# Mode weights turned to column order during the convolutions, and mixed as the moving operand

## The reference, cut to what matters

```python
# layer 0: three 3x3 convolutions whose weights are mixed per sample
x = x + conv3(conv2(conv1(gn(x))))     # w1..w3 = softmax(...) mix of 4 experts
# layer 1: a Hartley transform, cut to its middle 64 x 64 modes
X = dht2d(gn(x));  Xr = flip_periodic(X)          # h = Re fft2 - Im fft2
x_even, x_odd = (Xc + Xrc) / 2, (Xc - Xrc) / 2    # c: the middle 64 x 64
total = einsum('bixy,ioxy->boxy', x_even, weight) \
      + einsum('bixy,ioxy->boxy', x_odd, flip_periodic(weight))
x = x + dht2d(pad(total), inverse) + bias
```

## Time and profile before

| | |
|---|---|
| runs | 4752.64 us, median of 3 (4747.78 to 4760.87) |
| profiled execution | 4754.18 us; its span in the trace is 4752.4 us |
| convolutions | 0 to 3256 us |
| forward transform | 3257 to 3797 us |
| mixing | 3797 to 4056 us |
| inverse transform | 4056 to 4752 us |
| busy, share of the span | PE 91%, ACT 69%, DVE 61%, POOL 47% |
| HBM | read 746.67 MB, written 293.88 MB |

### The profile page before, as it was taken

One profiled execution on the slowest core, in us unless ns is written; L12 is line 12 of the kernel. 1 busy time (PEld: TensorE's weight loads), 2 busy tenths in 40 slices (PEclk: granted clock), 3 DMA queues, 4 the chain that ended last, 5 costly groups with the idle time before them and its releaser, 6 DMA issues. The chain is left out here.

```text
span 4752.4 us, 121017 instructions
## 1 busy us (share of the span) xinstructions
PE 4324.2 (91%) x40114; PEld 2695.9 (57%) x40114; DVE 2883.4 (61%) x4306; ACT 3292.8 (69%) x6385; POOL 2241.6 (47%) x2115
## 2 busy tenths in 40 slices
PE   4999999999999999999999999996677656899998
PEld 2555555454454555545555555454677656788887
DVE  4555555555555555555555555555699866565555
ACT  3888888888888888888888888884466567333333
POOL 4455454554545545455454554545799765000000
PEclk9999999999999999999999999998899978999999
DMA  4867768676686766867668676687999899899999
GB/s 136 198 153 180 171 150 198 153 180 169 151 197 152 180 168 151 197 153 180 167 153 199 155 179 163 157 198 208 301 320 323 272 205 205 336 409 411 409 404 378
DMA packets 717207, 1041.90 MB, mean 219 GB/s; under 512 B 151808, under 2 KB 599072, under 8 KB 667168
## 3 DMA queue, kind: packets, MB, share of 16 engines
q1 hardware_dynamic: 683296, 1032.09, 78.0%
q10 hardware_dynamic: 33792, 8.65, 1.0%
HBM read 746.67 MB, written 293.88 MB: 219 GB/s over the span
## 5 line engine op out<-in xcount | busy, mean ns | idle before, releaser
L350 PE MATMUL bank<-ring_B,w_now 128*64 128x512 f16 (+1 forms) x14283 | 3088.6, 377 | 58.3 <-DVE w_now L558 47.8
L350 PE MATMUL bank<-ring_A,w_now 128*64 128x512 f16 (+1 forms) x14283 | 3088.5, 377 | 0.0
L350 PEld LDWEIGHTS bank<-ring_B,w_now 128*64 128x64 f16 x14283 | 1551.6, 109 | 1484.0 <-DVE w_now L558 55.9
L350 PEld LDWEIGHTS bank<-ring_A,w_now 128*64 128x64 f16 x14283 | 1551.5, 109 | 52.5
L571 DVE SCALAR_TENSOR_TENSOR ring_A<-bank,ring_A 128x512 f16<-128x512 f32 (+1 forms) x1027 | 696.8, 678 | 1140.0 <-ACT ring_A L418 1119.9
L288 ACT COPY ring_B<-ring_A 64x516 f32<-64x516 f32 x1590 | 988.1, 621 | 503.0 <-DVE ring_A L571 434.3
L290 ACT COPY ring_B<-ring_A 64x516 f32<-64x516 f32 x1059 | 658.5, 622 | 12.3
L721 POOL TENSOR_TENSOR ring_A<-xn,ring_A 128x512 f16<-128x512 f32 x515 | 582.7, 1131 | 94.5 <-POOL xn L719 89.4
L418 ACT ACTIVATE ring_A<-bank 128x512 f16<-128x512 f32 (+1 forms) x1027 | 600.0, 584 | 35.7 <-PE bank L350 25.9
L1502 DVE SCALAR_TENSOR_TENSOR i_ot<-i_ob,i_bias_bc,i_xt 128x512 f32<-128x512 f32 x512 | 366.1, 747 | 288.0 <-DMA i_xt<-x 144.7
L1446 PE MATMUL i_ob<-i_back,i_u 128*128 128x256 f32 x2048 | 529.1, 381 | 7.9 <-DVE i_ot L1502 4.5
(11 more groups left out here) (163 smaller groups left out, 4982.0 us busy)
## 6 DMA issues: line engine op xcount, KB each, us to landing
f_xt<-x SPq DMA_DIRECT2D x128, 1024.0 KB, 6.9
i_xt<-x SPq DMA_DIRECT2D x128, 1024.0 KB, 16.0
out<-i_ot SPq DMA_DIRECT2D x128, 1024.0 KB, 14.2
st_in_A<-in_x SPq DMA_DIRECT2D x65, 1024.0 KB, 7.4
st_in_B<-in_x SPq DMA_DIRECT2D x65, 1024.0 KB, 7.9
x_in_A<-in_x SPq DMA_DIRECT2D x324, 192.0 KB, 3.9
res_A<-in_x SPq DMA_DIRECT2D x324, 192.0 KB, 5.2
res_B<-in_x SPq DMA_DIRECT2D x324, 192.0 KB, 5.1
```

The lines of the kernel that those rows point to most:

```text
L350: last = nc.tensor.matmul(dst[64 * half:64 * half + 64, 0:nb * IMG], w_now[n][:, w, 64 * dx:64 * dx + 64], r[side][:, kind, s0:s0 + nb, dx ...
```

## The change

Four parts.

1. In the convolutions, per sample s, SP loads four rows y of the weights (`w_rows`, in the tile `first`; four DMAs, each of 32 partitions and 32 pieces of 256 B per partition, 4096 pieces in all). DVE turns them to column order [x, o] by eight copies of 128 x 512 (four straight, in the inner loop at t = 5; four reversed, at t = 27, 28, 30, 31), and SP stores the two results to a DRAM tensor `turned` (two DMAs of 128 partitions, 8 KB pieces, 1 MB each). DVE waits once per sample, right after step 2, for all four loads.
2. The forward high parts are all made by ACT (two per group); ACT no longer copies half of y, and DVE copies both halves. The DRAM tensor `modes` is [2, 2, C, M/2, S, M]: the pieces of 256 B that SP stores lie 4 KB apart along a row index, where before they lay side by side.
3. The mixing loads `m_wt` directly from `turned` (16 DMAs of 32 partitions per chunk, 8 KB pieces), and `m_f_raw` in 16 KB pieces. The masked modes are the stationary operand and the weights the moving one. ACT and DVE build `m_ft`, one half each; POOL has no part; neither `m_raw` nor its copies exist. The result goes out in one DMA of 128 partitions with 8 KB pieces per chunk, by SP.
4. The inverse stage's constants are loaded by SP during chunk 3 of the mixing.

```diff
@@ build_convs, SyncE @@
             with sp.Fori(0, S) as s:
                 nxt = sp.snap((s + 1) % S)
                 n0 = sp.snap(s * NCH)
+                sp.wait_ge(turned, s * 8 + 1)
+                for j in range(4):
+                    sp.dma_start(w_rows[j * C:(j + 1) * C, :, 0:M], mode_w[:, :, bass.ds(s * 4 + j, 1), :].rearrange("i o a x -> i o (a x)")
+                                 ).then_inc(rows_here, 16)
...
                     load_stat(buf, nxt2, g - 1)
+                sp.wait_ge(turned, s * 8 + 9)
+                for i in range(2):
+                    sp.dma_start(turned_d[i, bass.ds(s * 4, 4)].rearrange("y i x -> (y i) x"), w_cols[i].rearrange("p x o -> p (x o)")
+                                 ).then_inc(turned_out, 16)
                 sp.wait_ge(x1_ready, n0 + NCH + 1)
@@ build_convs, VectorE @@
+            def turn_rising(i):
+                cols = bass.ds(i * 16, 16)
+                nc.vector.tensor_copy(w_cols[0][:, cols, :], w_rows[:, :, cols].rearrange("p o x -> p x o")).then_inc(turned, 1)
...
                 step(n0, 2, ("C", 0, s, None))
+                dve.wait_ge(turned_out, s * 32 + 1)
+                dve.wait_ge(rows_here, s * 64 + 64)
+                chain(nc.vector.tensor_copy(w_rows[:, :, M], w_rows[:, :, 0]), nb)
+                dve.sem_inc(passed, 1)
...
+                        if t == 5:
+                            turn_rising(i)
...
+                    if t in (27, 28, 30, 31):
+                        turn_falling((27, 28, 30, 31).index(t))
@@ load_weights @@
+    p = slice((2 * part + half) * C, (2 * part + half + 1) * C)
+    for t in range(ROWS):
+        r = ROWS * k + t
+        y = (M - r if half != part else r) if r else M // 2 * half
+        engine.dma_start(wt[p, t, :], turned_d[part, y]).then_inc(here, 16)
@@ build_forward @@
-        fv = f_d.rearrange("m t s (g c) r x -> m t s (c r) g x", c=4)
+        fv = f_d.rearrange("m t (g c) r s x -> m t s c r g x", c=4)
...
-                copy_y(nc.vector.tensor_copy, 0, g).then_inc(y_dve, 1)
+                nc.vector.tensor_copy(y_mid[:, :, 4 * g:4 * g + 4], made[:, :, :, NH - 1])
+                for wc in range(2):
+                    last = nc.vector.tensor_copy(y[buf][:, wc], made[:, wc, :, 0:M].rearrange("p c (t k) -> p t c k", t=2))
+                last.then_inc(y_ready, 1)
@@ build_forward, ScalarE @@
+                for j in range(2):
+                    part = lambda t: t[:, 2 * j:2 * j + 2, :].rearrange("p c w -> p (c w)")
+                    ch = 4 * g + 2 * j
+                    nc.scalar.activation(part(xh[g % NX]), part(xt[g % NX]), ACT.Copy, scale=scale_now[even][:, ch:ch + 1]
+                                         ).then_inc(hi_ready, 1)
@@ build_mix, SyncE @@
+            for k in range(NCK):
                 if k >= 2:
+                    sp.wait_ge(ft_dve, (k - 1) * NQ)
+                    sp.wait_ge(ft_act, (k - 1) * NQ)
+                load_modes(k)
+                if k >= 2:
+                    sp.wait_ge(made, (k - 1) * NQ)
+                    for part in range(2):
+                        for half in range(2):
+                            load_weights(sp, turned_d, k, part, half, wt[k % 2], w_here[k % 2])
+                    store(k - 2)
+                if k == 3:
+                    sp.dma_start(back[:], spec[:, OFF_BACK:OFF_BACK + 2 * IMG]).then_inc(consts_here, 16)
@@ build_mix, TensorE @@
-                    last = nc.tensor.matmul(bank[n % 2][:, x, :], wt[:, kx, :], ft[:, kx].rearrange("p t g b -> p (t g b)"),
+                    last = nc.tensor.matmul(bank[n % 2][:, x, :].rearrange("p (t o) -> p t o", t=T),
+                                            ft[:, kx].rearrange("p t g b -> p (t g b)"), wt[k % 2][:, :, kx * C:(kx + 1) * C],
                                             start=True, stop=True)
```

More of the change, by code:

```diff
@@ L127, in build_convs @@
         first = sb("first", [P, 8, 512 * 4])
+        spare = first[:].rearrange("p a b -> p (a b)")
+        w_rows = spare[:, 0:C * (M + 1)].rearrange("p (o x) -> p o x", o=C)
+        w_cols = [spare[:, 2048 * (2 + i):2048 * (3 + i)].rearrange("p (x o) -> p x o", o=C) for i in range(2)]
         bank = [[ps(f"bank{n}{i}", [P, 512]) for i in range(2)] for n in range(3)]
@@ L276, in _ @@
             sp.wait_ge(stored_stats, 16)
+            sp.wait_ge(turned_out, 32 * S + 1)
         def taps_view(m, n, dx):
@@ L1235, in _ @@
-                        sp.dma_start(to_rows(own, T - own), rows(T * k + own, T - own)).then_inc(f_here[buf], 16)
-                if k >= 2:
-                    sp.wait_ge(re_ready, (k - 1) * NQ)
-                    sp.wait_ge(im_ready, (k - 1) * NQ)
-                    for i in range(4):
-                        load_weights(sp, w, k, i, raw[buf], w_here[buf])
+                            sp.dma_start(f_raw[k % 2][p, 0], fm_d[:, :, part * M:(part + 1) * M].rearrange("b i x -> i b x")).then_inc(f_here[k % 2], 16)
@@ L1328, in _ @@
+            act.wait_ge(masks, 1)
             for n in range(NQ):
-                real(n)
+                modes(act, 1, n, multiply).then_inc(ft_act, 1)
             for n in steps:
-                take(act, nc.scalar.copy, (1, 2, 3), n, taken_act)
+                take(act, nc.scalar.copy, (2, 3), n, taken_act)
                 if n + NQ in steps:
-                    real(n + NQ)
-                if n >= NQ and n % NQ == 0:
-                    store(n // NQ - 1)
-            store(NCK - 1)
+                    modes(act, 1, n + NQ, multiply).then_inc(ft_act, 1)
@@ L1343, in _, with build_inverse @@
             last.then_inc(masks, 1)
-            pool.wait_ge(masks, 1)
-            for n in range(NQ):
-                modes(pool, nc.gpsimd.tensor_scalar, 0, n).then_inc(ft_pool, 1)
-            for n in steps:
-                if n + NQ in steps:
-                    pool.wait_ge(made, n + 1)
-                    modes(pool, nc.gpsimd.tensor_scalar, 0, n + NQ).then_inc(ft_pool, 1)
-def build_inverse(nc, t_d, x1d, bias, spec, out_d, S):
+def build_inverse(nc, t_d, x1d, back, bias_bc, out_d, S):
     f32 = mybir.dt.float32
@@ L1512, in build @@
     x1_stats = scratch("x1_stats", [P, S, 2])
[L1513 to L1515 removed]
+    modes, middle = scratch("modes", [2, 2, C, M // 2, S, M]), scratch("middle", [S, C, 2 * M])
+    mixed_modes = scratch("mixed_modes", [M // 2, 2, S, C, M])
+    turned = scratch("turned", [2, M, C, M * C])
+    build_convs(nc, x, w_c1, w_c2, weight1, weight2, weight3, mode_w, turned, consts, x1, x1_stats, S)
     with ExitStack() as ctx:
[L1518 to L1522 removed]
+        sb = lambda name, shape: ctx.enter_context(nc.sbuf_tensor(name, shape, f32))
+        back, bias_bc = sb("i_back", [P, 2 * IMG]), sb("i_bias_bc", [P, C])
+        with ExitStack() as inner:
+            wt = [inner.enter_context(nc.sbuf_tensor(f"m_wt{i}", [P, ROWS, M * C], f32)) for i in range(2)]
+            build_forward(nc, x1, x1_stats, spec, modes, middle, turned, wt, S)
+            build_mix(nc, modes, middle, turned, mixed_modes, wt, back, bias_bc, spec, bias, S)
+        build_inverse(nc, mixed_modes, x1, back, bias_bc, out, S)
 _INS = ["x", "L0_conv_w_c1", "L0_conv_w_c2", "L0_conv_weight1", "L0_conv_weight2", "L0_conv_weight3",
```

200 lines of the change are left out of this document (62 added, 138 removed).

## The result

The changed kernel takes 4897.97 us (median of 4 runs, 4891.78 to 4906.95) against 4750.21 for the kernel before on the same chip: ratio 1.0308, 95% interval 1.0284 to 1.0333. The forecast was 4807 us (range 4712 to 4900): the right side, but 57 us more were forecast where 148 us came. The execution that was profiled spans 4890.0 us, 137.6 more than before.

The account below looks back on a forecast made before the run. PE was taken to bound the convolutions, DVE and DMA the forward stage, DMA the mixing. 128 - 37 - 36 - 1 = +54 on 4754.2 gave 4808, less 1.5 for the median: 4807 us, range 4712 to 4900.

Parts of the forecast that it names:

- PE loses 8.4 - 1.9 = 6.5 us: Convolutions, each sample boundary: DVE's 8.1 us wait plus 0.3 for column copy and semaphore, less PE's 1.9 in hand.
- the new stretch at 1.2 GHz: Convolutions, after each boundary stop: 3.4 us of PE at the low clock, costing 1.7 us, taken once more.
- Rivals B and C: B: rows land before DVE wants them, 4684 us, chance 0.07; C: 256 B pieces cost like 1 KB, 5010 us, 0.08.
- The 5 us forecast behind the last sample: End of convolutions: the queue empties 5 us later, ahead of the forward stage; part of the +128 us.
- I charge nothing: Convolutions: the eight turning copies per sample, 0.47 to 0.92 us each, were taken to cost no time.
- the bound of 115: Convolutions: cost of the turning copies if nothing covers them, 128 x 0.9 = 115 us.
- The cover that was named: Convolutions: DVE's 1.9 us idle in a step and PE's 1.9 us in hand were to absorb the turning copies.
- the 3.29 us: Forward stage: DVE's time per group, 3.75 - 0.87 + 0.41; 3.42 was then taken as the period, giving -37 us.
- Rival D: Forward stage: `modes` stores 4 KB apart slow down; 4833 us at half rate, some 4950 at a quarter; chance 0.12.
- the walk: Mixing: chunk-by-chunk load times at 220 GB/s, 31.2 us per further chunk, ending at 4019 instead of 4056, -36 us.
- 64 matmuls at 0.13 us are 8.3 us: Mixing, tail: PE's work after the last loads, followed by two copies and a store with landing of 4.6 us.
- Rival A: Mixing and forward loads: piece size, not partitions, halved the rate; 8 KB pieces run at 401 GB/s; 4714 us, chance 0.15.

Follow-up runs that it names:

- late_wait: Changed kernel with VectorE's waits for turned stores and rows moved ahead of the first rising copy, column copy ahead of the falling ones: 4762.82 us, ratio 1.0025.
- late_gap: Changed kernel with row waits ahead of the first rising copy and all turning and column copies between the residual halves of their steps: 4701.69 us, ratio 0.9893.
- forward_alone: Kernel before, with both forward high parts made by ScalarE, y taken by VectorE alone and GpSimd idle there: 4711.82 us, ratio 0.9931.
- paired_rows: Changed kernel with late row waits, copies between residual halves, row loads behind eight turned stores, full-width mixing loads except chunk 0: 4602.39 us, ratio 0.9681.
- gap_copies: Changed kernel with each turning copy moved between the two residual halves of its step, waits unchanged: 4861.16 us, ratio 1.0233.
- rows_1k: Changed kernel with row loads in 1 KB instead of 256-byte pieces, rows landing wrongly in the partitions: 4879.22 us, ratio 1.0279.
- no_stores: Changed kernel with the two turned-weight stores made once behind the sample loop instead of per sample, output wrong: 4874.16 us, ratio 1.0262.

## Why the prediction was right or wrong

**Wait at the boundary: its length right by luck, TensorE's share too small.** 8.1 us were forecast for VectorE and 8.27 came, because two errors cancel. The rows land 15.1 us after `out_D` was issued, by forecast 13.6; but VectorE also ends step 2 later, 6.8 us after that point where it was 5.5 before. The transfer itself was well priced (6.3 us; 1.05 MB at 164 GB/s are 6.4). No row gave the 1 us taken for completion; here the DMA share falls to 0.10 at 2196.5, 1.6 us before the landing.

The failing step is "PE loses 8.4 - 1.9 = 6.5 us": TensorE is idle 8.2 us. VectorE's next statistic starts 8.97 us after the last one ended: 8.25 of wait, then 0.72 for the column copy and its semaphore, where 0.3 were forecast. That leaves 0.8 us of work in hand and not 1.9. TensorE had stopped once more just ahead, for a ring copy that follows an entry made by GpSimd; in the kernel before it is busy without a gap from 2066 to 2082. The two stops in the changed kernel:
```profile
2185.90 0.40 PE L365 MATMUL bank<-ring_B,w_now 128*64 128x512 f16 x1 [1.77 <-ACT ring_B L307]
2202.10 0.64 PE L365 MATMUL bank<-ring_B,w_now 128*64 128x512 f16 x1 [8.21 <-ACT ring_B L307]
```
How much of the missing 1.1 us the first stop explains was not taken apart. The clock was also thought of wrongly: the new stretch at 1.2 GHz (5.3 us of work, of which half is lost) does not come besides the old one but in its place, since the granted clock is 1.00 from 2175 to 2186. In the end the whole delay stays: from one `x1` (L610) to the next, the step with the wait takes 15.0 us, and 6.07 in `late_wait` (means of 14 boundaries). Removing the wait gave 9.0 us a boundary, 134.5 in all, where the forecast had 8.2 and 123. Rivals B and C are out with the wait of 8.3 us. The 5 us forecast behind the last sample can be seen: from the end of the issue of the last `out_D` to the first load of the forward stage it is 9.6 us, 3.7 before.

**Copies: "I charge nothing" was the larger failure.** With the stall out of the way the eight copies of a sample cost 57 us in all (3319.1 to 3261.8, some 6 of them the column copy's place in `late_wait`), half of the bound of 115; beside the stall they cost 33. The cover that was named is real, but stands ahead of the second `lo`, and the copies were put behind the step's last statistic, where the next step begins with one or two more. The four steps with a rising copy take 6.4 to 7.1 us in `late_wait` and 5.9 in `late_gap`. And the price of one came from L1300 in the mixing, not from the copies' own neighbours: beside GpSimd it is 1.25 us, above the range of 0.47 to 0.92. Sum of the stage, in this order of removal: 134.5 for the wait, 57.3 for the copies, 4.2 left: 196. In the other order it is 32.6 for the copies and 159.2 for the wait.

**Forward: -37 forecast, -39 measured.** The last 394 us of the stage hold 6402 matmuls, as many as the 424 us of the earlier trace rows, which were 113 groups; so a group takes 3.49 us (3.42 forecast):
```profile
3560.00:3954.00 394.00, 319.66 (x6402) 302.33 (x6401) 355.77 (x579) 324.15 (x615) 0.00 (x0) 0.95 0.98 339
```
These groups give 30 us and not 37; the other 9 come from the start of the stage, for which nothing was forecast, so the total is right partly by luck. So is the way to it: the 3.29 us start from the period of 3.75 as if VectorE never idled, but it was busy 389.14 / 113 = 3.44 us a group, and is 3.15 now. `forward_alone` shows that making the high parts on ScalarE carries 32 of the 39. Rival D is out: the stage runs at a DMA share of 0.96 and 320 GB/s, 297 before, with the stores of modes 4 KB apart.

**Mixing: -36 forecast, -21 measured; the mechanism right, the engine's term too small.** Chunk by chunk the walk nearly holds: TensorE gets the weights of chunks 2 to 7 at distances of 31.3 to 33.8 us, 160.7 in all where 159 were forecast, at 227 to 237 GB/s against 220. The step that failed is "64 matmuls at 0.13 us are 8.3 us". The window of the mixing above counts x128 in a chunk, as the earlier trace rows counted 512 in four: each of these matmuls is two records of 0.13 us. The end of the stage shows it, in the timeline of TensorE:
```profile
4170.12 16.14 PE L1264 MATMUL m_bank<-m_wt,m_ft 128*128 128x128 f32 x128 [12.00 <-DMA m_wt<-turned]
```
16.1 us in place of 8.3 make 8 of the missing us, which are 16 from the walk's own 4019 (that is -37; the sum took -36); 6 more are at the start, where the loads of the weights of chunk 2 wait for chunk 0's matmuls and are issued 32 us into the stage: TensorE gets them 55 us into it, 48 by forecast. Rival A is out (232 GB/s with 8 KB pieces). The 110 us that it held are there (`paired_rows` has 101 less than before the change in the mixing), but for partitions and not for the size of pieces.

**Inverse: the start right, the stage not.** The first matmul comes 6.5 us into the stage, 7.4 before; that is the forecast's 1 us. It waits for ScalarE's first copy of `i_t`; the forecast had named VectorE's as late next, and both start together behind a memset of VectorE. The whole stage is 1.4 us longer in this trace, and what takes the gain back stays open.

**The sum and the range.** In the traces 84 us are missing, 137.6 against 54: 68 in the convolutions, 15 in the mixing, 2 in the inverse, less 2 in the forward stage. 4897.97 us lies 2 us inside the range, and that is luck: the upper end had been raised from 4850 to 4900 for rival D, which did not happen. (In the earlier trace rows the clock falls at the starts of the forward stage and of the mixing, not in the middle of the span as the prediction reads it; nothing rests on that.)

## What to carry to other kernels

Put a new wait where the data are first needed, and a new instruction where its engine idles ahead of a later wait in the same step; a mean idle time says nothing about that place. Price a stop of the engine that bounds by the whole delay of the engine that feeds it: work in hand that was read in the old trace may be used up by another stop of the new kernel. Two costs that are taken away one by one need not add up; take away both. A wide load needs all partitions and a large outermost dimension on both sides (2 gave 53 GB/s here, 128 gave 430). And count an engine's work by records in the trace, not by calls in the code.

## What was not expected of the hardware

A VectorE copy from SBUF to SBUF took 0.61 us alone; when one of GpSimd's full-tile instructions had started before it, it ended 0.48 to 0.50 us after that one (1.23 to 1.45 us in the eight cases read). The Trainium skill (SBUF — State Buffer, "The single rule") speaks of a lock between the two that is held for a whole instruction; these rows agree. Three copies of `gap_copies` that started 0.05 to 0.11 us after a GpSimd instruction still took 0.61 to 0.65; that is open.

The same 4.2 MB of weights moved at 53 GB/s (outermost dimension 2), in a mix of 232 (32 partitions), 340 (weights over 128 partitions, modes over 32) and 430 GB/s (both over 128), all in pieces of 8 KB or more.

Between its last store of a sample and the first load of the next SyncE issued nothing for 5.5 us in the changed kernel, 5.6 in `rows_1k` and 4.1 in `no_stores`, with no wait in the code that was still open. In the changed kernel an instruction packet falls into that time; the DMA view from 2186.5 to 2187 us:
```profile
q1 hardware_dynamic: 35, 0.25, 123.5%
q14 instruction: 1, 0.01, 4.0%
```
That the loop's instructions came late behind the full queue would fit; no run tells it apart.
